# Self-attention on one Trainium2 core: value products issued two steps at a time, exponentials through three buffers, turned outputs through two

## The reference

```python
q = (x @ wq).reshape(B, T, H, D)
lat = x @ w_down
k = (lat @ wk_up).reshape(B, T, H, D)
v = (lat @ wv_up).reshape(B, T, H, D)
q = _apply_rope(q, cos, sin)
k = _apply_rope(k, cos, sin)
scores = jnp.einsum('bqhd,bkhd->bhqk', q, k) * scale
scores = jnp.where(allowed[None, None], scores, jnp.finfo(scores.dtype).min)
attn = jax.nn.softmax(scores, axis=-1)
out = jnp.einsum('bhqk,bkhd->bqhd', attn, v).reshape(B, T, E)
return out @ wo
```

## Time and profile before

| | |
|---|---|
| median of three runs | 823.99 us |
| the profiled execution | 824.24 us |
| its span in the trace | 822.5 us |
| PE busy | 755.3 us, 92% |
| DVE busy | 620.3 us, 75% |
| ACT busy | 427.4 us, 52% |
| self-attention's steps | from about 93 us to 531 us of the span |
| value products (L709) | 1280 MATMULs, 149.7 us of PE |

### The profile page before, as it was taken

How to read it: one execution, slowest core, us unless ns; L and a number is a source line. 1 busy time by engine, 2 the same in 40 slices (tenths; PEclk the granted TensorE clock), 3 DMA queues, 4 the chain that set the end, 5 groups by cost and what they waited for, 6 DMA issues and landing times. The chain is left out here.

```text
span 822.5 us, 12183 instructions
## 1 busy us (share of the span) xinstructions
PE 755.3 (92%) x4329; PEld 393.8 (48%) x4329; DVE 620.3 (75%) x1107; ACT 427.4 (52%) x879; POOL 149.9 (18%) x170
## 2 busy tenths in 40 slices
PE   8874887999999999999999998899868999999997
PEld 5431232333223333222333231287547888888886
DVE  4899687888998899999898760067614778778786
ACT  1552463676667776657777867822123333333353
POOL 2564000000000000000000000013141455555520
PEclk9986797999999999999999998999999999999999
DMA  7796321120000000000440000030001222222103
GB/s 209 207 266 202 87 76 39 33 59 27 1 2 2 1 2 2 1 2 0 158 142 1 2 0 2 3 110 1 0 1 41 80 81 80 80 80 80 40 1 103
DMA packets 27152, 47.32 MB, mean 58 GB/s; under 512 B 6112, under 2 KB 23008, under 8 KB 26336
## 3 DMA queue, kind: packets, MB, share of 16 engines
q1 hardware_dynamic: 25184, 43.94, 17.8%
q10 hardware_dynamic: 1920, 2.75, 1.2%
HBM read 38.16 MB, written 8.39 MB: 57 GB/s over the span
## 5 line engine op out<-in xcount | busy, mean ns | idle before, releaser
L486 DVE TENSOR_REDUCE part_max<-psum 128x1 f32<-128x512 f32 (+3 forms) x560 | 341.4, 669 | 55.0 <-PE psum L672 50.0
L591 ACT ACTIVATE probs<-psum 128x512 f32<-128x512 f32 (+3 forms) x640 | 293.7, 539 | 155.5 <-PE psum L697 154.5
L672 PE MATMUL psum<-k_stack,q_stack 96*128 96x512 bf16 (+4 forms) x640 | 214.9, 364 | 18.6 <-DVE psum L472 11.2
L697 PE MATMUL psum<-q_stack,k_stack 98*128 98x512 bf16 (+4 forms) x640 | 202.3, 357 | 13.1 <-DMA q_stack<-shift 11.3
L709 PE MATMUL psum<-probs,v_all 128*17 128x512 f32 (+3 forms) x1280 | 149.7, 540 | 0.3
L672 PEld LDWEIGHTS psum<-k_stack,q_stack 96*128 96x128 bf16 (+1 forms) x640 | 60.1, 99 | 171.9 <-DVE part_max L486 121.5
L697 PEld LDWEIGHTS psum<-q_stack,k_stack 98*128 98x128 bf16 (+1 forms) x640 | 60.9, 99 | 94.3 <-ACT probs L591 39.2
L1471 PE MATMUL psum<-ctx_part,qc_part 128*128 128x512 f32 (+1 forms) x384 | 84.7, 371 | 5.0 <-POOL qc_part L1253 4.1
L877 POOL MEMSET eps<- 128x4 f32 x1 | 0.1, 102 | 459.6 <-POOLq L273 459.6
L1545 PE MATMUL psum<-v_parts,p_part 128*128 128x512 f32 (+3 forms) x416 | 76.9, 341 | 0.0
L1471 PEld LDWEIGHTS psum<-ctx_part,qc_part 128*128 128x128 f32 x384 | 67.3, 192 | 18.9 <-issue 4.9
(11 more groups left out here) (140 smaller groups left out, 681.6 us busy)
## 6 DMA issues: line engine op xcount, KB each, us to landing
mask<-in_mask SPq DMA_DIRECT2D x16, 800.5 KB, 4.4
pieces<-k_stack SPq DMA_DIRECT2D x24, 256.0 KB, 5.0
q_stack<-pieces SPq DMA_DIRECT2D x24, 256.0 KB, 4.2
k_stack<-pieces SPq DMA_DIRECT2D x24, 256.0 KB, 4.7
x_sb<-in_x SPq DMA_DIRECT2D x4, 512.0 KB, 8.9
out<-x_sb SPq DMA_DIRECT2D x8, 256.0 KB, 2.2
q_stack<-in_ctxT SPq DMA_DIRECT2D x1, 1601.0 KB, 11.1
probs<-in_cos ACTq DMA_DIRECT2D x4, 256.0 KB
```

What stands on the lines that cost most here:

```text
L486: nc.vector.tensor_reduce(part_max[:, h:h + m, r, c:c + 1], src, axis=AX_X, op=ALU.max).then_inc(m_read, 1)
L591: nc.scalar.activation(probs[:, s % 2, h, col:BLK], s_bank[h][:, col:BLK], ACT.Exp, scale=ATTN_SCALE).then_inc(exp_done, 1)
L672: last = nc.tensor.matmul(out, q_stack[b][0:rows, g * G + h, r * P:(r + 1) * P], k_stack[c][0:rows, g * G + h, 0:keys], start=True, stop=True)
L697: nc.tensor.matmul(s_bank[h][:, col:BLK], k_stack[s // TPB][0:rows, g * G + h, (s % TPB) * P:(s % TPB + 1) * P], q_stack[b][0:rows, g * G ...
```

## The change

`weigh` is called in pairs. Of the list of steps, every second one (odd `i`) now issues two value products behind its scores, that of the step before last and that of the last; the even ones issue none. So that the exponentials of a step can wait for longer, `probs` has three buffers instead of two. To make room for it, `out_t` has two buffers instead of four, `warm` shares its place with the first `probs` buffer, and the weights `w_v` and `lat_t` of the first stage move from `out_t` into it. With two `out_t` buffers the copy L603 waits for the turn of the output two groups before, and the turning back of a block's last group goes into the second group of the next block instead of the third. The count and the shapes of all instructions stay as they are.

```diff
--- before.py
+++ after.py
@@ -121,8 +121,11 @@
 
     x, ident, v_all, attn = keep["x"], keep["ident"], keep["v_all"], keep["attn"]
     q_stack, k_stack = keep["q_stack"], keep["k_stack"]
-    probs = sb("probs", [P, 2, G, BLK])
-    out_t = sb("out_t", [P, NG, BLK])
+    with ExitStack() as same_place:
+        warm = same_place.enter_context(nc.sbuf_tensor("warm", [P, P + BLK], F32R))
+    PROBS, OUTS = 3, 2
+    probs = [sb(f"probs{n}", [P, G, BLK]) for n in range(PROBS)]
+    out_t = sb("out_t", [P, OUTS, BLK])
     part_max = sb("part_max", [P, G, TPB, NB])
     neg_max = sb("neg_max", [P, G * TPB])
     shift = sb("shift", [G * TPB, SHIFT_ROWS, P], BF16)
@@ -140,11 +143,12 @@
     piece = [whole((k_stack[2], k_stack[2], k_stack[3])[n])[:, n % 2 * 2 * half:(n % 2 + 1) * 2 * half]
              .rearrange("p (r u t) -> p r u t", r=2, u=4) for n in range(3)]
     xn_t = whole(k_stack[3]).bitcast(F32)[:, half:2 * half].rearrange("p (r c t) -> p r c t", r=2, c=EC)
-    cos, sin = (probs[:, n, :, :] for n in range(2))
+    cos, sin = (probs[n][:, :, :] for n in (1, 2))
+    behind_warm = probs[0][:, :, :].rearrange("p h t -> p (h t)")[:, P + BLK:]
     room = out_t[:, :, :].rearrange("p g t -> p (g t)")
     w_q = room[:, 0:EC * E].rearrange("p (c e) -> p c e", c=EC)
     w_lat = room[:, 512:512 + EC * P].rearrange("p (c e) -> p c e", c=EC)
-    w_k, w_v, lat_t = room[:, 768:1024], room[:, 1024:1280], room[:, 1280:1280 + BLK]
+    w_k, w_v, lat_t = room[:, 768:1024], behind_warm[:, 0:E], behind_warm[:, E:E + BLK]
     xn = attn
     stats = sb("stats", [P, TILES, 6])
     mv = sb("mv", [P, TILES, 2])
@@ -152,7 +156,6 @@
     rstd = sb("rstd", [P, TILES])
     minus_half = sb("minus_half", [P, TPB])
     eps = sb("eps", [P, TPB])
-    warm = sb("warm", [P, P + BLK], F32R)
 
     x_bank = [banks(psum, 0), banks(psum, 1)]
     lat_bank = banks(psum, 2)
@@ -229,7 +232,7 @@
     parts = [stream[:cut(-1)]]
     for k, (b, g) in enumerate(order):
         part = stream[cut(k - 1):cut(k)]
-        done = {NG - 2: [k - 2, k - 1] + ([k - 3] if b else []), NG - 1: [k - 1]}.get(g, [])
+        done = {1: [k - 2] if b else [], NG - 2: [k - 2, k - 1], NG - 1: [k - 1]}.get(g, [])
         for n, kk in enumerate(sorted(done)):
             part.insert(len(part) * (n + 2) // (len(done) + 2), ("out", kk, 0))
         parts.append(part)
@@ -583,12 +586,12 @@
             def step(b, g, s):
                 n = s_base(b, g) + s
                 col = first_col(b, s)
-                if n >= 2:
-
-                    act.wait_ge(pv_done, n - 1)
+                if n >= PROBS:
+
+                    act.wait_ge(pv_done, n - PROBS + 1)
                 for h in range(G):
                     act.wait_ge(s_ready, n * G + h + 1)
-                    nc.scalar.activation(probs[:, s % 2, h, col:BLK], s_bank[h][:, col:BLK], ACT.Exp,
+                    nc.scalar.activation(probs[n % PROBS][:, h, col:BLK], s_bank[h][:, col:BLK], ACT.Exp,
                                          scale=ATTN_SCALE).then_inc(exp_done, 1)
 
             def group(b, g):
@@ -598,9 +601,9 @@
                     step(*following(b, g), 0)
 
                 act.wait_ge(pv_done, s_base(b, g) + steps[b])
-                if b:
-                    act.wait_ge(o_turned, index(b, g) - NG + 1)
-                nc.scalar.activation(out_t[:, g, :], o_bank, ACT.Copy).then_inc(o_copied, 1)
+                if index(b, g) >= OUTS:
+                    act.wait_ge(o_turned, index(b, g) - OUTS + 1)
+                nc.scalar.activation(out_t[:, g % OUTS, :], o_bank, ACT.Copy).then_inc(o_copied, 1)
 
             step(0, 0, 0)
             for b in range(NB):
@@ -680,7 +683,7 @@
 
                         pe.wait_ge(o_copied, index(b, g) + 1)
                         for r in range(TPB):
-                            last = nc.tensor.transpose(bank[:, r * P:(r + 1) * P], out_t[:, g, r * P:(r + 1) * P],
+                            last = nc.tensor.transpose(bank[:, r * P:(r + 1) * P], out_t[:, g % OUTS, r * P:(r + 1) * P],
                                                        ident[:, :])
                         last.then_inc(m_ready, 1)
 
@@ -707,7 +710,7 @@
                     pe.wait_ge(o_copied, index(b, g))
                 for h in range(G):
                     last = nc.tensor.matmul(o_bank[32 * h:32 * h + VW, col:BLK], v_all[:, s, g * G + h, :],
-                                            probs[:, s % 2, h, col:BLK], start=s == 0, stop=s == steps[b] - 1)
+                                            probs[n % PROBS][:, h, col:BLK], start=s == 0, stop=s == steps[b] - 1)
                 last.then_inc(pv_done, 1)
 
             def group(b, g):
@@ -730,11 +733,15 @@
                         due = len(entries) * (sum(weights[:i]) + weights[i] * (h + 1) / (G + 1)) // sum(weights)
                         maxima(entries[done:int(due)])
                         done = max(done, int(due))
-                    weigh(b, g, s - 1 if s else steps[b] - 1)
+                    if i % 2:
+
+                        weigh(b, g, i - 1)
+                        weigh(b, g, i)
                     due = len(entries) * sum(weights[:i + 1]) // sum(weights)
                     maxima(entries[done:due])
                     done = max(done, due)
                 if not following(b, g):
+                    weigh(b, g, steps[b] - 2)
                     weigh(b, g, steps[b] - 1)
 
             pe.wait_ge(warm_ready, 1)
```

## The result

The changed kernel takes 841.69 us (median of 4 runs, 841.30 to 843.35); the kernel before, run beside it, takes 823.93. The ratio is 1.0217, with a 95% interval of 1.0197 to 1.0237: 2.2% slower, where 834.0 us had been forecast with a range of 826 to 844. The profiled span is 839.5 us, 17.0 longer than before.

The account below looks back on a forecast made before the run. PE was taken as the bound, with DVE right behind it nearly everywhere (ACT in the last group). From 824.24 us, +8.5 (windows), +5.1 (last group) and -3.5 (narrow pairs) gave 834.3, so 834 us; range 826 to 844.

Parts of the forecast that it names:

- The saved switch: At each pair of value products, the second pays no mode switch on PE: 0.20 us saved, bounds 0 and 0.22.
- the rival in which the second product pays again: At every pair: nothing saved and each absence 0.2 us longer, 846 us in all; chance 0.10.
- The longer absence: In wide steps, PE's time away from units grows from 1.29 to 2.15 us, starving DVE 0.84 us per pair; +8.5 us.
- The eleven windows: Stretches of full-width steps in groups (1,0) to (3,2), where the change makes pairs; forecast +8.5 us together.
- TensorE alone decides: Whole kernel: PE's savings of 0.20 us each count fully, 808 us, or 815 with a slower last group; chance 0.09.
- The last group: Group (3,3), scores without units: two steps take 4.75 us instead of 3.92, ACT idle some 0.8; +5.1 us.
- The narrow pairs: Group ends, products of 512 and 384 and of 256 and 128 queries: -0.3 us for each of 12 groups, -3.5 us.
- Buffers and places at zero: Third probs buffer, two out_t buffers, weights and lat_t in another place: taken to cost nothing.
- Block 0 at zero: Block 0, whose groups wait for maxima by DMA and not for value products: taken as unchanged.

Follow-up runs that it names:

- e1_buffers: Changed kernel without the pairs: three probs and two out_t buffers, moved turns and weights, one value product a step; 824.89 us, ratio 0.9996 to the kernel before.
- e6_half_before: Kernel before the change, with DVE's maxima over only half of each unit's columns; 804.75 us, ratio 0.9750 to the kernel before.
- e7_half_after: Changed kernel, with DVE's maxima over only half of each unit's columns; 797.76 us, ratio 0.9651 to the kernel before.
- e9_late_single: Changed kernel with each value product still a step late, but issued singly; 822.34 us, ratio 0.9966 to the kernel before.
- e3_wide_pairs: Changed kernel with pairs only where both steps are 512 wide, narrow ends single; 845.22 us, ratio 1.0246 to the kernel before.
- e4_only_32: Changed kernel with pairs only in the wide steps of group (3,2); 825.69 us, ratio 1.0011 to the kernel before.
- e12_late_again: The kernel of e9_late_single run once more, with more rounds; 820.15 us, ratio 0.9947 to the kernel before.

## Why it was right in sign and short in size

**The saved switch, as forecast.** 0.20 us had been taken per pair, with bounds of 0 and 0.22. The pair takes 1.84 us, 0.98 + 0.86 to the hundredth, and with DVE at ease each wide pair gains 0.21. This removes the rival in which the second product pays again.

**The longer absence: the gap as forecast, the sum partly by luck.** A gap of 0.84 us per pair was worked out from rows that held no pair; 0.85 is measured in (2,3). The eleven windows sum to +8.4 us against +8.5, but the single ones are up to 1.2 off and cancel. (2,1) and (3,1) are 0.9 and 1.2 longer than forecast, and (2,2) and (3,2) 0.9 shorter each, which is the moved turn of the output: e1_buffers has it in the same groups without any pair. I had put it at nothing, which holds for the whole and not for a window. Against e1_buffers the pairs cost the windows 10.7 us, and 11.9 without (1,0), whose clock was higher, where 8.9 had been forecast for these ten. So the term was right in kind, and the windows lost a third more than it says. (2,3), right to 0.25 us against before (31.77 for 32.01), is 2.95 longer than in e1_buffers, not 2.18. In (3,2) the pairs gain 0.64, and that is the forecast's 0.6.

**TensorE alone decides: refuted, with its condition.** Its 808 to 815 us need PE to be all that counts. e6_half_before and e7_half_after show that the wide pairs would behave just so if DVE's part were shorter, and the same edit is then a gain of 7 us. The two kernels differ from the real ones only in what DVE reduces. Together with e9_late_single, where the products are as late and nothing is lost, this shows the cause of the loss in the windows and doesn't only argue it.

The Trainium skill, "TensorEngine Tiling (Array Packing)", section "PSUM Bottleneck", says that tiling speeds up TensorE but not the emptying of PSUM. The trace agrees, with the 51.0 us of waits for banks above.

**The last group, mechanism right.** A cycle of 4.75 us with ACT idle for 0.8 was forecast; it is 4.77 and 0.74. The term was 5.1 and the trace has +4.2: the first cycle, 4.91 us where the same two steps took 5.43, gained 0.5 in place of costing 0.4, and the narrow end cost 0.3 in place of 0.5.

**The narrow pairs, the step that failed.** "PE gains 0.2 to 0.4 for a group, where DVE leaves it: I take -0.3 for each of 12 groups, -3.5 us (bounds 0 and -6)". The ends of the groups lost 3.4 us in place of gaining 3.5, outside both bounds, and this is most of the 7 us by which the forecast was low. Of the 3.4 us, 1.7 are there in e1_buffers without any pair, and belong to the moved turn; the pairs themselves cost 1.6. The prediction had named the sign of it: "A narrow end of the groups that doesn't gain would make it too low". (It also counted the last group among the twelve, though that had a term of its own for its end, and twelve times 0.4 is 4.8, not 6.) The timeline of all engines at the end of (3,0) after the change:

```profile
419.25 1.70 PE L712 MATMUL psum<-probs,v_all 128*17 128x512 f32 x16
...
421.20 2.96 ACT L594 ACTIVATE probs<-psum 128x128 f32<-128x128 f32 x8 [1.36 <-PE psum L700]
421.36 0.69 DVE L489 TENSOR_REDUCE part_max<-psum 128x1 f32<-128x512 f32 x1 [0.81 <-PE psum L675]
...
423.46 0.85 PE L712 MATMUL psum<-probs,v_all 128*17 128x256 f32 x16
```

DVE stands for 0.81 us here as well, not the 0.6 that I took. ACT stands for 1.36, since the scores of step 15 now stand behind the pair. The second narrow pair itself waits for nothing: it begins 0.31 us after the last unit (423.15 to 423.46), and step 15's exponentials had ended at 422.0 (the row of eight is these four and the four of the next group's first step). With DVE at ease the first narrow pair of (3,0) gains 0.18 us (4.37 to 4.19 us for its two steps, e6_half_before to e7_half_after), the second nothing (3.30 to 3.36), and over all eleven ends 0.3 us are lost. So even PE's 0.2 to 0.4 for a group was not there to be had; which wait takes it at each end is open. e3_wide_pairs adds that the loss can't be charged to the narrow pairs alone: take them away and it turns up in the next group. A sum that treats a group as one stretch, its DVE time plus all the gaps, would have avoided the split; it is argued here and wasn't tried.

**The rest.** Buffers and places at zero: right for the whole (e1_buffers). Block 0 at zero: it took 1.3 us more, a second, small part of the miss. The pairs aren't shown to be its cause: e3_wide_pairs and e4_only_32 have no pair in block 0, and it took 1.9 and 2.5 us more in them than in before.

What stays open: what takes the narrow pairs' saving, why the windows lose a third more than the gaps forecast, and where the part of the late single product's gain that isn't clock comes from.

## What to carry to other kernels

Putting like instructions together to save a change of mode also makes the engine absent for longer from whoever it feeds. Before doing it, set the longest absence (plus the delay to the consumer's start) against buffers times the consumer's time, and count the gap, not the shares: here 0.20 us was saved and a gap of 0.85 opened where two of up to 0.35 had been, and with a lighter consumer the same edit wins. A buffer that is bought for a merged step may pay better when it only lets single steps run late. And a group of steps is priced as a whole: what its end seems to save can be lost at the start of the next.

## What the hardware showed that I had not expected

The stretches of low clock moved between executions whose matmuls stand in the same order. e9_late_single and e12_late_again are one kernel; from 123 to 153 us their granted clock was 0.77 and 0.83, and their block 0 took 146.1 and 143.1 us. In e4_only_32 it was 0.66, and 0.77 in e1_buffers, where the order up to there is the same; (0,3) and (1,0) were 1.2 and 1.3 us longer for it. So two executions of the same order of work can differ by 1 to 3 us in these groups, and a local gain of 0.7 us, as in (3,2), is then not to be measured over the whole.
